# Fused image and text embedding, windowed attention and mixture of experts: products two slots later, routing in the next step, image rows earlier and partly on GpSimd

## The chip, the cores and the metric

The kernel runs on one core of a Trainium2 chip. The metric is device time in microseconds (us). Three runs of the kernel before gave 1399.01, 1400.30 and 1402.45 us, so the median is 1400.3 us. All profile times below are of one other execution, taken by the hardware profiler.

## The reference, cut to what matters

```python
h = clip(|x[i,j]-x[i+1,j+1]| + |x[i+1,j]-x[i,j+1]|, 0, 1)   # 16 images of 256 rows x 256
h = concat([h, table[x_txt]], axis=1)                       # + 77 text rows: S = 333 tokens of 256
h = h + attention(layernorm(h))                             # fp32 in, 16 heads of 16
h = h + experts(layernorm(h))                               # 8 experts, the 2 best, SwiGLU 256-512-256
```

The attention works on windows of 128 tokens at a stride of 64: four regular windows, and a fifth that ends at the last token. Each window has its own softmax over 128 keys with a position bias. The results of the windows that cover a token are added and divided by their number, and go through `Wo`. The experts take all 16 x 333 tokens together, sorted by expert.

## The kernel before

There are two stages. The **attention stage** goes over the 16 batches in steps: step `b` runs the attention of batch `b`, and beside it the projections of batch `b+1` (`proj`), the image, the text rows and the first layer norm of batch `b+2` (`inp`), the output projection, residual and second layer norm of batch `b-1` (`tail`), and the routing of batch `b-2` (`tail2`). The **expert stage** afterwards goes through 91 tiles of 128 sorted rows.

A step has 20 slots `k`: five windows times four groups of four heads. The order of the work is written out by hand. Every engine has its own function `step(b, par)` with a loop over `k`, in which lines such as `if proj and k == 4:` put a piece of side work into a slot. Engines run their own list strictly in order and meet at semaphores. A group goes through:

- PE, slot k: four score products of group k into `s_bank` (L1026); they need the row maxima of group k-2. At k = 0 the engine waits for `stack_in`, the landing of the batch's Q and K stacks.
- DVE, slot k: bias and row maximum of group k (L757, four instructions).
- ACT, slot k: exponential of group k-1 (L622), and then the copy of the transposed probabilities of group k-2 out of `t_bank` (L636). For every fourth group DVE makes that copy (L772, with the `weight` copy L776).
- PE, slot k: transpose of the probabilities of group k-3 (L1040), and their product with V for group k-4 (L1063). After a window's last group it transposes `weight` (L1072); ACT copies it (L642), DVE multiplies it into `head_out` (L784), and POOL adds that to `ctxT` (L520).

`probsT` has two buffers.

The Q and K stacks carry a chain of their own, from one step to the next. PE transposes the normalised rows `xn` of batch b+1 at k = 0 (L1082), ACT copies them (`xT`, L648), PE makes Q in slots 2 and 3 and K in slots 4 and 5 (L1104), and ACT takes each half out (`qk`, L660). Each of Q (n = 0) and K (n = 1) is then split into three bf16 parts: DVE rounds the first part (`part_high(n)`, L733), POOL subtracts (`split_rest(n)`, L502), DVE rounds the second (`part_middle(n)`, L738), and POOL subtracts again for the third (`split_last(n)`, L507). SP writes the parts to DRAM (L366) and reads them back, stacked by the products that are wanted, into `stacks` (L372): `load_stack(0)` for Q and `load_stack(1)` for K, six transfers of 166.5 KB each. SP's list is in order too:

```python
write_part(0, 2, part3_ready)
write_part(1, 1, part2_ready)
load_stack(0, q_stack[par1], Q_SLOTS)     # waits for all parts of Q in DRAM
write_part(1, 2, part3_ready)
if tail: store_h2()
load_stack(1, k_stack[par1], K_SLOTS)     # waits for all parts of K in DRAM
```

then four shifts inside V (L392 to L396), and the next step's image rows (L343 to L347).

Other side work that the texts name: `add_v` on DVE (L745, V out of PSUM), `moments_of` on DVE (L706 and L709, statistics of a layer norm, once for `inp` and once for `tail`), `inverse_root` on POOL (L472 to L484), `normalise` on DVE (L714, which makes `xn` for `inp`), the image's two differences on POOL (L533, L536) and their absolute values on DVE (L851), the sum and the clip on DVE (L870, L875), the output projection on PE (L1004) with the residual on DVE (L856), and the routing: gate product on PE (L1142), best two on DVE (L903 to L910), one-hot rows (L790 to L805), prefix sum on PE (L1089), places (L827 to L841) and scores (L812 to L819) on DVE, and six indirect scatters by POOL (L493).

## Time and profile before

| | |
|---|---|
| median of three runs | 1400.3 us (1399.01 to 1402.45) |
| profiled execution | 1394.69 us, span 1392.9 us |
| first scores of step 0 / step 1 / step 2 / step 15 | 63.43 / 116.21 / 162.03 / 786.04 us |
| first product of the expert stage | 872.3 us |
| busy over the span | PE 85%, DVE 66%, ACT 56%, POOL 44% |
| mean granted TensorE clock | 0.919 of full |

The span runs from the first to the last instruction. Times in the profile are from the span's start; the execution's own time is 1.8 us more than its span. L12 is line 12 of the kernel before. PEld is TensorE's weight load, which overlaps its products. SPq is the queue of transfers that SP issues. A bracket behind a row, as in [2.06 <-DMA stacks], is the idle time of the engine just before the row, and what ended it.

### The profile page before, as it was taken

Reading aid. Unit: us, or ns where it says so; the run is one execution under the profiler, and the core shown is the slowest. Engines: PE = TensorE matmul, PEld = TensorE weight load, DVE = VectorE, ACT = ScalarE, POOL = GpSimd, SP = SyncE. Lnnn points to the kernel's source line nnn. Section 1 sums busy time; section 2 is a strip of 40 time slices with the busy share of each in tenths; the row PEclk is TensorE's granted clock in tenths of the full one; section 3 lists DMA queues with packets and bytes.
Section 4 is the critical chain, followed back from the end, with each engine's and each line's share of the span. In section 5 each row is a group of like instructions: output and inputs, shape, how many; then the busy total and the mean of one; then the engine's idle time right before and its main releaser. Section 6 shows DMA issues by size and latency. Waiting matters only on the chain.

```text
span 1392.9 us, 35049 instructions
## 1 busy us (share of the span) xinstructions
PE 1189.1 (85%) x10190; PEld 951.8 (68%) x10191; DVE 920.9 (66%) x4211; ACT 782.9 (56%) x3176; POOL 611.8 (44%) x900
## 2 busy tenths in 40 slices
PE   2386888988988998888889872999999999999996
PEld 1254656655655665555556551999999999999995
DVE  4485989888888889898997864344444444444442
ACT  0196998989899998899899980211111111111110
POOL 5333466565646655665665334122322232232232
PEclk9698899889898988999998985899999999999998
DMA  3694563465357446634643507232233323323222
GB/s 110 133 234 100 109 132 89 95 131 113 88 103 142 92 92 116 128 89 94 133 107 71 96 24 234 36 50 46 49 47 48 49 45 49 48 46 48 46 49 31
DMA packets 98402, 123.36 MB, mean 89 GB/s; under 512 B 15544, under 2 KB 87416, under 8 KB 95192
## 3 DMA queue, kind: packets, MB, share of 16 engines
q1 hardware_dynamic: 75880, 89.96, 30.6%
q0 software_dynamic: 18576, 24.47, 10.9%
q10 hardware_dynamic: 3808, 7.34, 1.8%
q8 instruction: 57, 0.93, 0.3%
q14 instruction: 81, 0.66, 0.2%
HBM read 69.35 MB, written 46.07 MB: 83 GB/s over the span
## 4 chain that ended last, share of the span: by engine, by line
PE 47%; POOL 16%; issue 14%; DMA 12%; ACT 4%; SPq 3%; DVE 3%; POOLq 0%; DVEq 0%; ACTq 0%
PE s_bank L1168 12%; PE t_bank L1168 12%; PE o_bank L1183 11%; DMA qk_parts<-parts_flat 5%; POOL expert_slots L493 4%; DMA expert_slots<-rows,slot_i 4%; DMA stacks<-qk_parts 3%; PE m_bank L1104 3%; ACT probs L622 3%; PE t_bank L1040 2%; SPq L372 2%; POOL rest L502 2%; PE o_bank L1063 2%; POOL parts_flat L507 2%; PE m_bank L1157 1%
## 5 line engine op out<-in xcount | busy, mean ns | idle before, releaser
L622 ACT ACTIVATE probs<-probs,neg_max 128x128 f32<-128x128 f32 x1280 | 497.4, 401 | 21.6 <-DVE neg_max L757 21.0
L757 DVE CUSTOM_DVE_ANT_0 probs<-s_bank,nbias 128x128 f32<-128x128 f32 x1280 | 293.0, 284 | 38.4 <-PE s_bank L1026 36.9
L622 ACT ACTIVATION_READ_ACCUMULATOR probs<-probs,neg_max 128x1 f32 x1280 | 257.4, 201 | 0.0
L1040 PE MATMUL t_bank<-ident,probs 128*128 128x128 f32 x1280 | 221.0, 300 | 28.7 <-ACT probs L622 26.7
L681 ACT ACTIVATE v_all<-s_bank 128x512 f32<-128x512 f32 x91 | 54.4, 598 | 286.9 <-PE s_bank L1168 286.9
L1026 PE MATMUL s_bank<-stacks 96*128 96x128 bf16 x1280 | 136.5, 233 | 68.8 <-DMA stacks<-qk_parts 46.9
L1026 PEld LDWEIGHTS s_bank<-stacks 96*128 96x128 bf16 x1280 | 93.4, 105 | 132.4 <-DMA stacks<-qk_parts 50.7
L1040 PEld LDWEIGHTS t_bank<-ident,probs 128*128 128x128 f32 x1280 | 150.1, 153 | 45.7 <-ACT probs L622 41.7
L636 ACT ACTIVATE probsT<-t_bank 128x512 f32<-128x512 f32 x240 | 141.9, 591 | 57.5 <-PE t_bank L1040 56.7
L1183 PE MATMUL o_bank<-stacks,v_all 128*128 x728 | 172.6, 380 | 0.7 <-issue 0.5
L597 POOL DMA_INDIRECT out_dram<-wq_sb,nbias x46 | 75.7, 1645 | 198.5 <-DVE wq_sb L967 185.3
L1063 PE MATMUL o_bank<-probsT,v_all 128*32 128x128 f32 x2560 | 146.0, 303 | 16.9 <-ACT probsT L636 9.7
L597 POOL DMA_INDIRECT out_dram<-wk_sb,nbias x45 | 73.3, 1629 | 172.8 <-DVE wk_sb L967 170.0
L973 DVE TENSOR_TENSOR v_all<-v_all,t_bank 128x512 f32<-128x512 f32 x91 | 62.6, 688 | 127.1 <-PE t_bank L1168 127.1
L1183 PEld LDWEIGHTS o_bank<-stacks,v_all 128*128 128x128 f32 x728 | 131.3, 190 | 16.0 <-issue 1.8
L675 ACT ACTIVATE v_all<-m_bank 128x256 f32<-128x256 f32 x91 | 35.0, 384 | 143.3 <-PE m_bank L1157 143.3
L493 POOL DMA_INDIRECT expert_slots<-rows,slot_i x96 | 100.0, 1042 | 29.3 <-issue 21.7
L1063 PEld LDWEIGHTS o_bank<-probsT,v_all 128*32 128x32 f32 x2560 | 52.9, 112 | 79.0 <-issue 50.0
L757 DVE DVE_READ_ACCUMULATOR2_ANT neg_max<- 128x1 f32 x1280 | 103.8, 81 | 0.1
L1168 PEld LDWEIGHTS s_bank<-v_all,probs 128*128 128x128 f32 x736 | 91.0, 195 | 3.2 <-ACT v_all L675 0.9
L1168 PE MATMUL s_bank<-v_all,probs 128*128 128x128 f32 x736 | 91.4, 278 | 0.5 <-ACT v_all L675 0.5
L1168 PE MATMUL t_bank<-v_all,probs 128*128 128x128 f32 x736 | 90.7, 277 | 0.0
(158 smaller groups left out, 2079.4 us busy)
## 6 DMA issues: line engine op xcount, KB each, us to landing
stacks<-qk_parts SPq DMA_DIRECT2D x192, 166.5 KB, 5.6
qk_parts<-parts_flat SPq DMA_DIRECT2D x192, 83.2 KB
nbias<-expert_slots SPq DMA_DIRECT2D x91, 129.0 KB, 2.0
w_sb<-in_L_ffn_w_dram ACTq DMA_DIRECT2D x14, 512.0 KB, 5.2
v_all<-v_all SPq DMA_DIRECT2D x64, 96.0 KB, 6.4
x_here<-in_x_dram SPq DMA_DIRECT2D x16, 256.0 KB, 5.7
out_dram<-h_res SPq DMA_DIRECT2D x16, 256.0 KB
stacks<-in_L_ffn_w_dram SPq DMA_DIRECT2D x8, 512.0 KB, 8.5
```

What stands on the lines that cost most here:

```text
L493: pool.indirect_dma_start(slots_dram[:, :], bass.IndirectOffsetOnAxis(slot_i[0:n, kk, j:j + 1], 0), rows[0:n, kk, j, :], None).then_inc(sc ...
L597: pool.indirect_dma_start(out[:, :], bass.IndirectOffsetOnAxis(g_rows[r][:, D + 1:D + 2].bitcast(I32), 0), y_sb[r], None, compute_op=ALU.a ...
L622: ins = act.activation(seg, seg, ACT.Exp, bias=neg_max[:, r, i:i + 1], scale=-1.0, accum_out=row_sum[:, (par + v) % 2, h:h + 1])
L636: act.activation(probsT[:, k % 2, :], t_bank[:, k % 2, :], ACT.Copy).then_inc(pT_by_act, 1)
L681: act.activation(hidT[r % 2], s_bank[:, r % 2, :], ACT.Silu).then_inc(silu_ready, 1)
L757: ins = dve.tensor_tensor_reduce(probs[:, r, i * WIN:(i + 1) * WIN], s_bank[:, k % 2, i * WIN:(i + 1) * WIN], nbias[:, h, :], 1.0, BIG, AL ...
L973: dve.tensor_tensor(hidT[r % 2], hidT[r % 2], t_bank[:, r % 2, :], ALU.mult).then_inc(hid_ready, 1)
L1026: mm = pe.matmul(s_bank[:, k % 2, i * WIN:(i + 1) * WIN], q_stack[par][0:KROWS, h, lo:lo + WIN], k_stack[par][0:KROWS, h, lo:lo + WIN], st ...
L1040: mm = pe.transpose(t_bank[:, (k - 3) % 2, i * WIN:(i + 1) * WIN], probs[:, r, i * WIN:(i + 1) * WIN], ident[:, :])
L1063: mm = pe.matmul(o_bank[32 * i:32 * i + 32, vp, (g // 2) * WIN:(g // 2 + 1) * WIN], v_win[bp][:, w, c0:c0 + 2 * HD], probsT[:, (k - 4) % 2 ...
L1168: mm = pe.matmul(bank[:, par, n * P:(n + 1) * P], up_w[par][:, m, a, n * P:(n + 1) * P], gxT[par][:, a * P:(a + 1) * P], start=(a == 0), s ...
L1183: mm = pe.matmul(o_bank[:, r % 2, 0:D], hidT[r % 2][:, a * P:(a + 1) * P], w2_sb[:, bass.ds(e, 1), a, :].rearrange("p o n -> p (o n)"), st ...
```

## The change

It touches only the order of the attention stage, four buffers and two loads:

- The copies: ACT copies group k-3 at the head of slot k, ahead of the exponential of group k-1; DVE's copy of every fourth group moves one slot later, to the head of its slot. The product with V takes group k-6 instead of k-4. `probsT` has four buffers; the two new ones lie in the memory of the `w3` weights of expert 6, whose load moves from step 0 to the end of the attention stage. `head_out` and the `ctxT` additions move with the products.
- The routing of batch b-2: the gate product goes from slot 18 to slot 3 of the next step, the rest from slots 19, 0, 2, 3 to slots 4 (best two), 6 (one-hot rows), 9 (places) and 10 (scores); the scatters from slots 4 to 9 to slots 11 to 13.
- The image of batch b+2: POOL's differences at slots 0 and 1 instead of 2 and 3, DVE's absolute values at 2 instead of 7, sum and clip on POOL at 3 instead of on DVE at 11, moments at 5 instead of 15, the root at 12 instead of 16, `xn` at 16 instead of 18.
- The projections: the parts of Q and K one to two slots later, V directly behind K on PE (slots 6 and 7 instead of 10 and 11) and on DVE (8 and 9 instead of 12 and 14), the output projection at 10 and 11 instead of 6 and 7, residual, second layer norm and `x2T` two to four slots later.
- SP: the V shifts ahead of `load_stack(1)`, the store of h2 behind it.

```diff
-        probsT = sb("probsT", [P, 2, GH * WIN])
+        probsT2 = sb("probsT", [P, 2, GH * WIN])
+        probsT = [probsT2[:, i, :] for i in range(2)] + [w3_sb[:, E - 2, c, :] for c in range(C)]
...
                     load_stack(0, q_stack[par1], Q_SLOTS)
                     write_part(1, 2, part3_ready)
-                    if tail:
-                        store_h2()
-                    load_stack(1, k_stack[par1], K_SLOTS)
                     vt = v_win[par1]
...
                     sp.dma_start(vt[64:128, 3, :], vt[o:o + 64, 4, :]).then_inc(v_shift_in, 16)
+                    load_stack(1, k_stack[par1], K_SLOTS)
+                    if tail:
+                        store_h2()
...
+                    if inp and k == 3:
+                        pool.wait_ge(conv_step, b2 * 3 + 2)
+                        pool.tensor_tensor(diag[:, :, :], diag[:, :, :], anti[:, :, :], ALU.add).then_inc(conv_step, 1)
...
+                        pool.tensor_scalar(h_in[par][:, 0:2, :], diag[:, :, :], 1.0, 0.0, ALU.min, ALU.max)\
+                            .then_inc(image_ready, 1)
+                    if proj and k == 6:
+                        split_rest(0)
-                    if proj and k == 5:
-                        split_rest(0)
...
-                    if proj and k == 7:
+                    if proj and k == 8:
                         split_last(0)
                         split_rest(1)
...
-                    if proj and k == 9:
+                    if proj and k == 10:
                         split_last(1)
...
+                    g = (k - 3) % NG
+                    if g != 3 and ((k >= 3 and att) or (k < 3 and tail)):
+                        n = b * G + (k - 3)
+                        act.wait_ge(pT_done, n + 1)
+                        if n >= 4:
+                            act.wait_ge(pv_done, n - 3)
+                        act.activation(probsT[n % 4], t_bank[:, n % 2, :], ACT.Copy).then_inc(pT_by_act, 1)
                     if (k >= 1 and att) or (k < 1 and tail):
...
-                    if proj and k == 4:
+                    if proj and k == 5:
                         part_high(0)
-                    if proj and k == 6:
+                    if inp and k == 5:
+                        dve.wait_ge(image_ready, b2 + 1)
+                        dve.wait_ge(text_in, b2 * 16 + 16)
+                        if b2 >= 1:
+                            dve.wait_ge(rstd1_ready, b2)
+                        moments_of(h_in[par], stats1, moments1, b2, ln1_step)
+                    if proj and k == 7:
                         part_high(1)
+                    if proj and k == 8:
                         part_middle(0)
...
-                    if proj and k == 8:
+                    if proj and k == 10:
                         part_middle(1)
...
-                    if inp and k == 18:
+                    if inp and k == 16:
                         dve.wait_ge(rstd1_ready, b2 + 1)
...
-                    if (k >= 4 and att) or (k < 4 and tail):
+                    if (k >= 6 and att) or (k < 6 and tail):
 
-                        m, n = k - 4, b * G + (k - 4)
+                        m, n = k - 6, b * G + (k - 6)
...
-                    if tail and k == 18:
-                        pe.wait_ge(x2T_ready, b0 + 1)
-                        pe.wait_ge(head_ready, min(b * NW + 3, B * NW))
+                    if tail2 and k == 3:
+                        pe.wait_ge(x2T_ready, b9 + 1)
+                        pe.wait_ge(head_ready, min(b * NW - 1, B * NW))
```

On DVE the place that matters lies between the first rounding of K and its second. The rows are of the kernel before; each "..." stands for eight rows of the row maxima.

```order
L733 CAST parts_flat<-qk 128x2x333
L738 CAST parts_flat<-rest 128x2x333
...
L851 TENSOR_SCALAR diag<-diag 128x512
L851 TENSOR_SCALAR anti<-anti 128x512
...
L784 TENSOR_TENSOR head_out<-o_bank,weightT 128x256
L856 SCALAR_TENSOR_TENSOR h_res0<-m_bank,inv_count,h_res0 128x256 x2
L856 SCALAR_TENSOR_TENSOR h_res0<-m_bank,inv_count,h_res0 77x256
L738 CAST parts_flat<-rest 128x2x333
```

And the same place with the change, where lines are those of the changed kernel (L744 is `part_high`, L749 `part_middle`, L756 `add_v`, L850 and L854 begin the places, which go on over three more small rows, and L835 to L842 are the scores):

```order
L744 CAST parts_flat<-qk 128x2x333
...
L749 CAST parts_flat<-rest 128x2x333
L756 TENSOR_TENSOR v_all<-m_bank,bv_row 128x8x2x16 x2
...
L850 TENSOR_TENSOR place<-o_bank,region_end 128x24
...
L756 TENSOR_TENSOR v_all<-m_bank,bv_row 128x8x2x16
...
L790 RECIPROCAL inv_sum<-row_sum 128x16
L797 TENSOR_TENSOR head_out<-o_bank,weightT 128x256
L835 TENSOR_REDUCE score_sum<-score_e 128x3
...
L749 CAST parts_flat<-rest 128x2x333
```

Between the two roundings of K there were two groups of row maxima and now there are three; the V rows, the places and the scores have come in between, and the absolute values and the residual have gone.

On SP, the tail of the list of a step before:

```order
L372 DMA stacks<-qk_parts 16x5328 x6
L366 DMA qk_parts<-parts_flat 8x16x333 x2
L357 DMA out_dram<-h_res0 128x2x256
L358 DMA out_dram<-h_res0 77x256
L372 DMA stacks<-qk_parts 16x5328 x6
L392 DMA v_all<-v_all 64x384
```

and with the change:

```order
L373 DMA stacks<-qk_parts 16x5328 x6
L367 DMA qk_parts<-parts_flat 8x16x333 x2
L390 DMA v_all<-v_all 64x384
L391 DMA v_all<-v_all 64x384
L392 DMA v_all<-v_all 64x384
L394 DMA v_all<-v_all 64x384
L373 DMA stacks<-qk_parts 16x5328 x6
L358 DMA out_dram<-h_res1 128x2x256
```

The V shifts and the store of h2 have changed sides of the K stack.

## Rows read from the trace of the kernel before

**Rows 1.** Busy time by engine, attention stage (columns: us, busy, clock, DMA share, GB/s)

```profile
160.00:760.00 600.00, 525.76 (x4972) 359.79 (x4964) 528.16 (x2973) 539.38 (x2332) 353.18 (x598) 0.90 0.51 106
```

**Rows 2.** First scores of steps 1, 7, 8 and 15, PE in order of time

```profile
116.21 0.61 PE L1026 MATMUL s_bank<-stacks 96*128 96x128 bf16 x4 [12.46 <-DMA stacks<-qk_parts]
...
400.63 0.61 PE L1026 MATMUL s_bank<-stacks 96*128 96x128 bf16 x4 [1.36 <-DMA stacks<-qk_parts]
...
449.23 0.61 PE L1026 MATMUL s_bank<-stacks 96*128 96x128 bf16 x4 [2.06 <-DMA stacks<-qk_parts]
...
786.04 0.61 PE L1026 MATMUL s_bank<-stacks 96*128 96x128 bf16 x4 [1.73 <-DMA stacks<-qk_parts]
```

**Rows 3.** SP's queue in order of time, step 7

```profile
427.89 2.72 SPq L372 DMA_DIRECT2D stacks<-qk_parts  x6
430.65 1.22 SPq L366 DMA_DIRECT2D qk_parts<-parts_flat  x2
...
438.98 4.10 SPq L372 DMA_DIRECT2D stacks<-qk_parts  x6
```

**Rows 4.** The two stretches behind those issues, columns as in group 1

```profile
428.00:439.00 11.00, 8.49 (x87) 5.46 (x86) 10.97 (x59) 9.38 (x43) 6.66 (x18) 0.94 0.92 171
439.00:449.00 10.00, 8.09 (x86) 5.76 (x84) 7.91 (x46) 10.00 (x45) 5.68 (x17) 0.84 0.87 147
```

**Rows 5.** DVE in order of time, step 7

```profile
399.78 2.56 DVE L714 TENSOR_SCALAR xn<-h_in,moments,rstd 128x256 f32<-128x256 f32 x3 [2.10 <-POOL rstd L484]
...
411.85 0.18 DVE L827 TENSOR_TENSOR place<-o_bank,region_end 128x24 f32<-128x24 f32 x1
...
412.73 0.29 DVE L757 CUSTOM_DVE_ANT_0 probs<-s_bank,nbias 128x128 f32<-128x128 f32 x1
...
425.65 0.92 DVE L738 CAST parts_flat<-rest 128x666 bf16<-128x666 f32 x1 [0.37 <-POOL rest L502]
...
429.83 0.28 DVE L757 CUSTOM_DVE_ANT_0 probs<-s_bank,nbias 128x128 f32<-128x128 f32 x1
...
430.67 1.07 DVE L706 BATCH_NORM_STATS2 stats<-h_res 128x6 f32<-128x256 f32 x3
431.67 0.29 DVE L709 BATCH_NORM_AGGREGATE moments<-stats 128x2 f32<-128x6 f32 x3
```

**Rows 6.** PE in order of time, step 7, and the first of the expert stage

```profile
403.96 1.37 PE L1082 MATMUL m_bank<-ident,xn 128*128 128x128 f32 x6
...
422.14 0.61 PE L1040 MATMUL t_bank<-ident,probs 128*128 128x128 f32 x4
...
423.27 0.61 PE L1040 MATMUL t_bank<-ident,probs 128*128 128x128 f32 x4
...
444.25 1.33 PE L1142 MATMUL o_bank<-gate_sb,rest 128*128 128x8 f32 x12
...
871.17 0.66 PE L1157 MATMUL m_bank<-ident,nbias 128*128 128x128 f32 x2 [15.66 <-DMA nbias<-expert_slots]
```

**Rows 7.** DVE's groups, 160 to 760 us (busy us, mean ns of one; idle before)

```profile
L772 DVE COPY probsT<-t_bank 128x512 f32<-128x512 f32 x62 | 41.2, 664 | 22.5 <-PE t_bank L1040 22.2
L784 DVE TENSOR_TENSOR head_out<-o_bank,weightT 128x256 f32<-128x256 f32 x62 | 26.1, 421 | 9.3 <-ACT weightT L642 9.3
...
L745 DVE TENSOR_TENSOR v_all<-m_bank,bv_row 128x256 f32<-128x256 f32 x36 | 13.9, 414 | 0.0
```

**Rows 8.** Granted clock at the seam between steps and in slots 2 to 9

```profile
399.00:406.00 7.00, 4.36 (x31) 3.37 (x31) 6.15 (x34) 4.92 (x21) 3.10 (x5) 0.58 0.48 119
407.00:424.00 17.00, 17.00 (x168) 11.70 (x164) 13.69 (x85) 16.85 (x73) 10.62 (x10) 1.00 0.21 59
```

**Rows 9.** Waits by engine, 160 to 760 us (us in total, times, longest)

```profile
ACT probsT L636 <- PE t_bank L1040: 39.6, 50, 2.1
...
DVE xn L714 <- POOL rstd L484: 26.4, 13, 2.3
```

**Rows 10.** Software queue of transfers, 160 to 760 us

```profile
q0 software_dynamic: 4183, 9.58, 6.0%
```

More of the change, by code:

```diff
@@ L749, in step @@
                 for k in range(G):
+                    v = (k - 7) // NG
+                    if (k - 7) % NG == 0 and ((att and v >= 0) or (tail and v < 0)):
+                        n, wv, vp = b * G + (k - 4), b * NW + v, (par + v) % 2
+                        dve.wait_ge(pT_done, n + 1)
+                        if n >= 4:
+                            dve.wait_ge(pv_done, n - 3)
+                        dve.tensor_copy(probsT[n % 4], t_bank[:, n % 2, :]).then_inc(pT_by_dve, 1)
+                        dve.wait_ge(inv_ready, wv + 1)
+                        if wv >= 2:
+                            dve.wait_ge(weightT_done, wv - 1)
+                        dve.tensor_copy(weight[:, vp, :, :], inv_sum[:, vp, :].unsqueeze(2).to_broadcast([P, H, HD]))\
+                            .then_inc(weight_ready, 1)
                     if att:
@@ L785, in step @@
                             .then_inc(head_ready, 1)
-                    if tail2 and k == 0:
+                    if tail2 and k == 4:
+                        dve.wait_ge(logits_done, b9 + 1)
+                        dve.tensor_copy(logits[:, :, :], o_bank[:, par, 0:NT * E].rearrange("p (j e) -> p j e", j=NT))\
+                            .then_inc(logits_read, 1)
+                        dve.wait_ge(logits_read, b9 + 1)
+                        for j in range(NT):
+                            dve.max(best[:, j, :], logits[:, j, :]).then_inc(best_ready, 1)
+                        for j in range(NT):
+                            dve.wait_ge(best_ready, b9 * 6 + 1 + j)
+                            dve.max_index(best_i[:, j, :], best[:, j, :], logits[:, j, :]).then_inc(best_ready, 1)
+                    if tail2 and k == 6:
                         if b9 >= 1:
@@ L806, in step @@
                             .then_inc(taken_ready, 1)
-                    if tail2 and k == 2:
+                    if tail2 and k == 10:
                         dve.wait_ge(score_e_ready, b9 + 1)
@@ L822, in step @@
                         dve.wait_ge(token_step, b9 + 1)
-                    if tail2 and k == 3:
-                        counted = o_bank[:, par, 0:(NT + 1) * E]
+                    if tail2 and k == 9:
+                        counted = o_bank[:, 1 - par, 0:(NT + 1) * E]
                         dve.wait_ge(prefix_done, b9 + 1)
@@ L1083, in step @@
                         mm.then_inc(xT_done, 1)
-                    if tail2 and k == 2:
-                        counted = o_bank[:, par, :]
+                    if tail2 and k == 8:
+                        counted = o_bank[:, 1 - par, :]
                         pe.wait_ge(taken_ready, b9 + 1)
-                        pe.wait_ge(head_ready, min(b * NW - 1, B * NW))
+                        pe.wait_ge(head_ready, min(b * NW, B * NW))
                         pe.matmul(counted[:, 0:NT * E], before[:, :], taken[:, :, :].rearrange("p j e -> p (j e)"),
@@ L1106, in step @@
                         mm.then_inc(qk_done, 1)
-                    if tail and k == 6:
+                    if proj and k == 6:
+                        pe.wait_ge(qk_ready, b1 * 4 + 3)
+                        v_proj(0, 0, 0)
+                    if proj and k == 7:
+                        v_proj(0, D, 2)
+                        pe.wait_ge(qk_ready, b1 * 4 + 4)
+                        v_proj(1, 0, 4)
+                    if tail and k == 10:
                         pe.wait_ge(ctx_added, b0 * NW + NW)
                         if proj:
-                            pe.wait_ge(qk_ready, b1 * 4 + 3)
+                            pe.wait_ge(v_ready, b1 * 3 + 3)
                         elif b0 >= 1:
```

195 lines of the change are left out of this document (74 added, 121 removed).

## The prediction

> **What bounds the kernel now.** Read the attention stage first, as busy time by engine [rows 1]: of 600 us ACT is busy 539, DVE 528, PE 526. No engine is full, though each is within a tenth or so of it, and none names the bound. Next, who waits [rows 9]: ACT waits 39.6 us for transposes, DVE 26.4 us for the root on POOL. These invite the view that the engines are too tightly coupled, which is what longer distances and more buffers would cure. Then PE in order of time at the steps' seams [rows 2]: in the steps shown the first scores are released by the landing of the Q and K stacks, after 1.4 to 2.1 us idle, and 14 steps take 786.04 - 116.21 = 669.8 us, 47.85 each. The step's length is thus also that of a chain which runs from one seam to the next: xT, Q and K, their parts, the parts in DRAM, the stacks. In step 7 (from 400.63, 48.6 us long) its stations are, counted from the seam:
>
> - second rounding of K (`part_middle(1)`) ends on DVE at 425.65 + 0.92 = 426.57, so +25.9 [rows 2, 5];
> - the Q stack is issued at 427.89, so +27.3, which is 1.3 behind the rounding (the write of that part stands between) [rows 3];
> - the K stack is issued at 438.98, 11.1 us later [rows 3]; it waits for the last part of K, which is written behind the six Q transfers;
> - the next first scores are at 449.23, 10.25 us later [rows 2].
>
> In the last two stretches the transfer engines are 0.92 and 0.87 busy [rows 4]. From the Q stack on, the chain is therefore made of bytes: 11.1 + 10.25 = 21.3 us that no compute engine shortens. What the step can gain or lose through the chain, it gains or loses ahead of the Q stack, at `part_middle(1)`.
>
> **The change, part by part.** The question is when `part_middle(1)` ends, counted from a seam at which PE has waited for the stack and the other engines have caught up.
>
> *The start.* Before, `xn` is being normalised across the seam (until 402.34, 1.7 behind it) [rows 5], and PE's transposes of `xn` start at +3.3 [rows 6]. With the change `xn` is made in slot 16 and its root in slot 12; the 26.4 us of waits for the root (2.1 a step) go [rows 9]. I start xT at +2.0, 1.3 earlier. That is not all of the 3.3, since scores, transposes and product of slot 0 still stand ahead of it, and at the seam TensorE has its lower level of clock for part of the time: mean 0.58 of full against 1.00 in slots 2 to 9, of its two levels of 1.2 and 2.4 GHz [rows 8]. ACT, though, now has a `weight` transpose of PE's slot 1 to wait for ahead of its xT copy, so I expect only 0.5 to 1 us of it to reach Q.
>
> *PE up to slot 5.* A slot without side work costs PE 423.27 - 422.14 = 1.13 us [rows 6]. The gate product, 1.33 us [rows 6], now stands in slot 3, ahead of both halves of K. What was gained at the start is given back here: I put the scores of slot 5 at +13 (if the seam is at full clock) to +15 (at the lower level for slots 0 and 1).
>
> *DVE from slot 5 to `part_middle(1)`.* This is the term that counts. One group of maxima costs 430.67 - 429.83 = 0.84 us [rows 5]. Six of them (slots 5 to 10) are 5.0. Two roundings each of first and second parts at 0.5 are 2.0 (the row shows 0.92 for one beside a POOL subtraction) [rows 5]. The moments of the next image, new here, are 1.07 + 0.29 = 1.3 [rows 5]. The places of the routing, new here, take 412.73 - 411.85 = 0.9 [rows 5]; the one-hot rows and the scores, eleven small rows more, I estimate at 2.2 from that. V's three additions are 3 x 0.41 = 1.2, two head products 0.8 with two reciprocals of a quarter us, and one copy of `probsT` 0.66 [rows 7] with its small `weight` copy. That is 5.0 + 2.0 + 1.3 + 0.9 + 2.2 + 1.2 + 1.3 + 0.9 = 14.8, and 15.4 us with a few waits. So `part_middle(1)` ends at +28.4 to +30.4. I take +29.5, nearer the upper end since the seam of [rows 8] is at the lower clock, against +25.9: **3.6 us a step later**. The lower bound of the whole is 13 + 14.8 = 27.8, with no wait at all, 1.9 a step; the upper 30.9, with another half us of contention with POOL, 5.0. Less than that would take DVE or PE work away that the list still has there.
>
> *Behind it.* `split_last(1)` follows on POOL, which is freer than before since the scatters have gone behind it; its last part is written behind the Q stack in any case, so nothing is gained. SP's exchange of V shifts (4 x 96 KB) against h2 (333 KB) ahead of the K stack puts 51 KB more in front, about 0.3 us at 147 GB/s [rows 4]. I leave it in the range.
>
> *Covered.* Sum and clip on POOL take 1.15 us off DVE per step and cost POOL some 2 us in slot 3, where it has nothing due until slot 6. The longer distance of the products and the later copies remove ACT's waits for transposes [rows 9], 39.6 us in 12.5 steps, 3.2 a step, and DVE's for the root; but a step that is held by its stacks only turns them into a longer wait at its seam. If that cover goes, they are the gain of the first rival. The load of `w3` of expert 6 (0.5 MB) behind the stage joins 5 MB of expert weights that load beside the last routing; the expert stage starts on the landing of its token rows, not of its weights [rows 6]: nothing.
>
> *Sum.* 14 steps x 3.6 = +50. Step 15 prepares no batch and may gain its share of the waits: -1. On 1394.7 us, the profiled execution's own time, that is 1443.7; the median of the runs stands 5.6 higher, so I predict **1449 us**.
>
> **The rivals.**
>
> *A, the coupling was the bound (faster).* The stacks land in time and ACT sets the step: 539.4 of 600 us busy [rows 1] is 43.0 of 47.85, with 1.5 us of residual waits 44.5. 14 x -3.35 = -47: 1353 us. It decides if K's stack lands by +44.5, that is, if `part_middle(1)` ends before 44.5 - 21.3 - 1.3 = +21.9. For it: every engine has a tenth idle, and the root's wait is real. Against it: the rounding stands behind three groups of maxima and the routing instead of two. Chance 0.10.
>
> *B, no net change.* The earlier xT and the undisturbed DVE make up for the two slots, `part_middle(1)` stays near +25.9: 1400 us. Chance 0.05.
>
> *C, the scatters as well (slower still).* Six scatters move from slots 4 to 9 into slots 11 to 13, so into the two stretches that are 0.9 full [rows 4]; before, two of six lay there. Their queue takes 6.0% of all transfer engines [rows 10], 36 us in 12.5 steps, 2.9 a step with the text rows, some 0.45 per scatter. Four more are +1.8 us a step: 1449 + 25 = 1474 us. The Trainium skill (DMA: Bandwidth & Descriptors, section on queues, rings and completion order) says that each transfer engine takes turns between the queues that have work for it, a packet at a time. By that rule the scatters slow the stacks at once and are not served behind them; no row of the kernel before shows the two apart. Chance 0.25.
>
> *D, the forecast:* chance 0.60.
>
> **How the numbers follow.** The time is that of D. About 0.3% (4 us) is what a measurement of this kernel can tell from no change. A gives faster 0.10 and B a little of each side: faster 0.11, same 0.04, slower 0.85. The range takes D's bounds, 14 x 1.9 - 1 and 14 x 5.0 - 1 (1426 to 1469), C up to 1480, and below a part of B: 1410 to 1480. What is left out is A, half of B, and the end of C.
>
> **What would show it.** Right: every step's first scores released by the stacks, after more idle than 1 to 2 us; steps of 50 to 53 us; `part_middle(1)` ending at +28 to +31; Q stack to K stack still about 11 us and K stack to seam about 10; no wait of DVE for the root; ACT, DVE and PE less busy in share. Wrong: steps shorter than 47 us, or the first scores released by something other than a transfer. C would show as more than 22 us from the Q stack to the seam.

## The result and the profile after

The changed kernel takes **1460.6 us** (median; 1458.0 to 1463.6) against 1400.1 us before (median of four runs here; 1399.0 to 1402.5): a ratio of **1.043**, 95% interval 1.040 to 1.046. Slower, as forecast, and 11.6 us above the forecast of 1449. The profiled execution took 1461.98 us with a span of 1460.2; against the one before that is 67.3 us more, and all sums below are made against that.

The page of the kernel after, busy time by engine (PE's share includes the expert stage), and three of its rows of queues:

```profile
PE 1205.2 (83%) x10190; PEld 968.5 (66%) x10191; DVE 879.6 (60%) x4179; ACT 782.9 (54%) x3176; POOL 625.8 (43%) x932
...
q0 software_dynamic: 18576, 24.47, 10.9%
...
q8 instruction: 57, 0.93, 0.3%
q14 instruction: 81, 0.66, 0.2%
```

The attention stage, as in [rows 1]:

```profile
160.00:760.00 600.00, 496.07 (x4586) 344.20 (x4586) 457.18 (x2710) 498.18 (x2154) 332.34 (x572) 0.88 0.46 98
```

Every engine is less busy than in [rows 1], and so are the transfers (0.46 against 0.51): the same work per step is spread over a longer step, and the stage waits more. Where the time lies is read from PE in order of time, beside [rows 2] and the last of [rows 6]. First scores of steps 1, 7 and 8, those of slot 5 of step 7 between them, the first scores of step 15, and the first expert product:

```profile
117.51 0.61 PE L1030 MATMUL s_bank<-stacks 96*128 96x128 bf16 x4 [15.86 <-DMA stacks<-qk_parts]
...
424.68 0.61 PE L1030 MATMUL s_bank<-stacks 96*128 96x128 bf16 x4
...
437.50 0.39 PE L1030 MATMUL s_bank<-stacks 96*128 96x128 bf16 x4
...
476.31 0.61 PE L1030 MATMUL s_bank<-stacks 96*128 96x128 bf16 x4 [0.81 <-DMA stacks<-qk_parts]
...
840.78 0.40 PE L1030 MATMUL s_bank<-stacks 96*128 96x128 bf16 x4
...
938.89 0.45 PE L1157 MATMUL m_bank<-ident,nbias 128*128 128x128 f32 x1 [15.85 <-DMA nbias<-expert_slots]
```

The 67.7 us by which the expert stage begins later are 1.3 at the first seam, 723.3 - 669.8 = 53.4 in 14 steps (3.8 each), and 98.1 - 85.1 = 13.0 from the first scores of step 15 to the first expert product. From there to the end it is 521.3 us after and 521.7 before. (A seam is the moment at which a step's first scores begin.) Of the twelve seams at which steps 2 to 13 begin, seven show no wait of PE for a stack at all, as the one at 424.68. In the kernel before it was already five of twelve; [rows 2] has only seams with a wait.

What else holds them is seen in step 7, on four queues. SP's, beside [rows 3]:

```profile
454.31 2.71 SPq L373 DMA_DIRECT2D stacks<-qk_parts  x6
...
466.07 3.33 SPq L373 DMA_DIRECT2D stacks<-qk_parts  x6
```

DVE's, beside [rows 5]: second rounding of K, moments of the rows, and the rows themselves:

```profile
452.49 0.51 DVE L749 CAST parts_flat<-rest 128x666 bf16<-128x666 f32 x1
...
459.35 0.30 DVE L720 BATCH_NORM_AGGREGATE moments<-stats 128x2 f32<-128x6 f32 x3
...
465.99 1.11 DVE L725 TENSOR_SCALAR xn<-w_sb,moments,rstd 128x256 f32<-128x256 f32 x3
...
470.77 1.44 DVE L725 TENSOR_SCALAR rows<-h_res,moments,rstd 128x256 f32<-128x256 f32 x3 [2.26 <-POOL rstd L487]
```

POOL's: the last of the six scatters, then first and last instruction of the rows' root:

```profile
465.74 0.96 POOL L496 DMA_INDIRECT expert_slots<-rows,slot_i  x1 [0.30 <-issue]
466.76 0.38 POOL L475 TENSOR_SCALAR var_eps<-moments 128x3 f32<-128x3 f32 x1
...
470.54 0.19 POOL L487 TENSOR_TENSOR rstd<-rstd,root_tmp 128x3 f32<-128x3 f32 x1
```

And PE's transposes of the rows, in slot 18:

```profile
472.26 1.37 PE L1134 MATMUL m_bank<-ident,rows 128*128 128x128 f32 x6 [2.92 <-DVE rows L725]
```

Counted from the seam at 424.68: last rounding done at +28.3, stacks issued at +29.6 and +41.4, the next seam at +51.6. But the moments were ready at +35.0, and their root began only at +42.1: on POOL it stands behind three scatters, the next images' root (3.9 us) and three scatters more. Of the 7.1 us between, the images' root took the first part (it had begun at +34.4, when the first three scatters were off) and the last three scatters the rest. Rows at +46.1, transposes at +47.6, 4 us before the seam. That is a **second chain of almost the same length**, and it comes out in the waits of the stage:

```profile
DVE probs L780 <- PE s_bank L1030: 96.6, 96, 5.6
...
PE m_bank L1134 <- DVE rows L725: 32.8, 11, 5.3
ACT probsT L629 <- PE t_bank L1044: 31.6, 33, 3.6
...
DVE rows L725 <- issue: 20.3, 5, 4.9
...
ACT weightT L653 <- remote: 16.5, 7, 2.6
DVE rows L725 <- POOL rstd L487: 13.3, 6, 2.6
...
PE s_bank L1030 <- DMA stacks<-qk_parts: 8.8, 5, 5.2
```

Of [rows 9], DVE's wait for the root ahead of `xn` is gone. In its place DVE stands at the rows, 33.6 us in all, PE behind it for 32.8, and the stacks account for 8.8 alone. The 20.3 us with the releaser "issue" show no partner; the last experiment shows what they are.

### The profile page after: what moved, and what is told of

The parts are those of the page before. It is cut to its first block, busy times and chain, and to the rows that moved or that the text cites. A ratio compares the mean times of both kernels' runs of the same rounds, so it can differ in the third digit from the quotient of the medians.

```text
span 1460.2 us, 35047 instructions
## 1 busy us (share of the span) xinstructions
PE 1205.2 (83%) x10190; PEld 968.5 (66%) x10191; DVE 879.6 (60%) x4179; ACT 782.9 (54%) x3176; POOL 625.8 (43%) x932
## 4 chain that ended last, share of the span: by engine, by line
PE 56%; POOL 11%; issue 11%; ACT 6%; DMA 6%; DVE 5%; SPq 4%; another core or an unknown queue 1%; ACTq 0%; POOLq 0%; DVEq 0%
PE s_bank L1168 11%; PE t_bank L1168 11%; PE o_bank L1183 11%; PE t_bank L1044 5%; PE m_bank L1108 4%; POOL expert_slots L496 4%; ACT probs L638 4%; PE o_bank L1067 3%; DMA stacks<-qk_parts 3%; DMA qk_parts<-parts_flat 3%; PE m_bank L1015 3%; PE s_bank L1030 2%; SPq L373 2%; PE m_bank L1157 1%; PE o_bank L1142 1%
## 5 line engine op out<-in xcount | busy, mean ns | idle before, releaser
L1044 PE MATMUL t_bank<-ident,probs 128*128 128x128 f32 x1280 | 230.9, 310 | 64.9 <-ACT probs L638 60.1
L1044 PEld LDWEIGHTS t_bank<-ident,probs 128*128 128x128 f32 x1280 | 156.9, 159 | 85.2 <-ACT probs L638 77.0
L1030 PE MATMUL s_bank<-stacks 96*128 96x128 bf16 x1280 | 140.8, 238 | 55.4 <-DMA stacks<-qk_parts 49.2
L1030 PEld LDWEIGHTS s_bank<-stacks 96*128 96x128 bf16 x1280 | 100.0, 107 | 105.7 <-DMA stacks<-qk_parts 53.5
L629 ACT ACTIVATE probsT<-t_bank 128x512 f32<-128x512 f32 x160 | 94.9, 593 | 68.3 <-PE t_bank L1044 55.5
L496 POOL DMA_INDIRECT expert_slots<-rows,slot_i x96 | 96.6, 1006 | 37.8 <-issue 29.2
L510 POOL TENSOR_TENSOR parts_flat<-rest,parts_flat 128x666 bf16<-128x666 f32 x32 | 45.2, 1412 | 110.5 <-DVE parts_flat L749 110.5
L1168 PEld LDWEIGHTS s_bank<-v_all,parts_flat 128*128 128x128 f32 x720 | 87.4, 192 | 3.0 <-ACT v_all L686 0.7
```

The costliest lines, as they stand in the source:

```text
L496: pool.indirect_dma_start(slots_dram[:, :], bass.IndirectOffsetOnAxis(slot_i[0:n, kk, j:j + 1], 0), rows[0:n, kk, j, :], None).then_inc(sc ...
L629: act.activation(probsT[n % 4], t_bank[:, n % 2, :], ACT.Copy).then_inc(pT_by_act, 1)
L1030: mm = pe.matmul(s_bank[:, k % 2, i * WIN:(i + 1) * WIN], q_stack[par][0:KROWS, h, lo:lo + WIN], k_stack[par][0:KROWS, h, lo:lo + WIN], st ...
L1044: mm = pe.transpose(t_bank[:, n % 2, i * WIN:(i + 1) * WIN], probs[:, r, i * WIN:(i + 1) * WIN], ident[:, :])
L1168: mm = pe.matmul(bank[:, par, n * P:(n + 1) * P], up_w[par][:, m, a, n * P:(n + 1) * P], gxT[par][:, a * P:(a + 1) * P], start=(a == 0), s ...
```

## The experiments

Theory S (the prediction's): the chain to the stacks sets the step, and the roundings lengthened it. Theory T: the tail does, that is product with `Wo`, residual, moments, root, rows, transposes in slot 18. For orientation, the means over steps 2 to 13 of each kernel in us, from its timeline, counted from the seam (the last rounding is `part_middle(1)`; "K to seam" goes from the issue of K's stack to the next seam):

```text
kernel                         step  last rounding  K stack  K to  rows' root  rows
                                      ends           issued  seam  starts      start
before                         48.0   25.9           38.2     9.8  31.4        38.0
after                          51.9   28.7           41.3    10.6  42.5        47.3
before, roundings late         49.8   27.5           40.1     9.7  30.0        35.6
before, routing late           52.9   28.6           41.9    11.0  34.8        45.0
before, images ahead           47.0   24.3           37.4     9.6  29.8        36.2
after, roundings early         50.8   23.0           36.3    14.4  40.1        46.5
after, root in slot 14         52.3   28.2           41.3    11.0  38.1        48.0
after, root in slot 8          51.9   29.0           42.0     9.9  39.9        46.9
  and roundings early          51.2   24.1           36.7    14.5  40.9        47.2
after, routing early           48.2   25.9           38.9     9.4  36.7        40.6
  and roundings early          46.6   22.6           36.2    10.4  35.6        39.6
  and images as before         46.3   23.1           36.4     9.9  35.4        40.1
  or scatters late again       51.2   22.2           35.4    15.8  37.6        44.0
```

**1. The roundings alone, on the kernel before.**

```diff
-                    if proj and k == 4:
+                    if proj and k == 5:
                         part_high(0)
...
-                    if proj and k == 8:
+                    if proj and k == 10:
                         part_middle(1)
```

(`part_high(1)` 6 to 7, `part_middle(0)` 6 to 8; GpSimd's slots 5, 7, 9 to 6, 8, 10.)

> The kernel before with one thing of the change alone: the roundings of Q and K one to two slots later on DVE (first parts in slots 5 and 7, second parts in 8 and 10) and the subtractions on GpSimd in slots 6, 8, 10; nothing else moves. Theory S (the step is set by the chain to the stacks, and its loss is the two slots of the last rounding): part_middle(1) ends at about +30 instead of +25.9, Q stack at about +31.5, each step 3.5 to 4.5 us longer, 1450 to 1463 us. Theory T (the step after the change is set by the tail: product with Wo, moments, root on GpSimd, rows, transposes of rows in slot 18): the tail of this kernel is where it was, so the Q and K stacks only come later into slack: under 1 us a step, 1400 to 1414 us.

Measured: 1423.4 us, ratio 1.016 (1.013 to 1.019). It falls between the two bands: the direction is S's, the size less than half. PE now stands at each seam for its stack:

```profile
PE s_bank L1027 <- DMA stacks<-qk_parts: 69.3, 12, 6.8
```

With 5.8 us of waiting at the seam the next step begins with everyone caught up: xT starts at +2.0 instead of +3.2 and the scores of slot 5 at +12.4 instead of +13.7, and the two slots cost 1.7 us at the last rounding, not the 4.8 of two slots of 48.0 / 20 us.

**2. The roundings back, in the kernel after.** The same edit the other way.

> The kernel after with the roundings of Q and K and their subtractions back in the slots of before (4, 6, 6, 8 on DVE and 5, 7, 7, 9 on GpSimd), the rest as changed. S: part_middle(1) ends 3 to 4 us earlier, near +25.5, and the step follows: 47.5 to 48.5 us, 1401 to 1416 us. T: the stacks land early, but TensorE still stands at the transposes of the rows in slot 18 and the step keeps at least 50.5 us: 1445 to 1461 us. If both chains are nearly equally long, the step falls by only part of it, to 49.5 to 50.5: 1430 to 1444 us.

Measured: 1434.6 us, 1.025 (1.022 to 1.028); 26 us of the loss, in the band for two chains of about one length. The last rounding ends at +23.0 and K's stack is issued at +36.3, so by the 9.4 to 9.9 us that it takes where a stack releases the seam it has landed at +46, yet the seam comes at +50.8. The same waits as above:

```profile
PE m_bank L1134 <- DVE rows L725: 65.0, 11, 6.7
...
DVE rows L725 <- issue: 66.8, 10, 7.3
```

At the twelve seams that end its steps 2 to 13 PE never waits for a stack. The tail alone holds this kernel at 50.8. S by itself is refuted.

**3. The next images' root moved behind the rows' root** (GpSimd, slot 12 to slot 14), without and with the early roundings.

```diff
-                    if inp and k == 12:
+                    if inp and k == 14:
...
                         inverse_root(moments1, rstd1, root1_step, b2, rstd1_ready)
```

> The kernel after with one move: the root for the next images (GpSimd, slot 12) put behind the root for the rows (slot 14), so that the rows' root stands behind 3.8 us less of GpSimd work. S: the wait of the transposes in slot 18 (34.4 us in 12.5 steps) falls under 15, but the first scores wait for the stacks instead: 1455 to 1461 us. T: the step falls by 1 to 2 us, 1432 to 1447 us.

> Both of the moves: roundings back in their slots of before and the next images' root behind the rows' root. S: as with the roundings alone, within 5 us. T: as with the root alone, within 5 us. Two chains of nearly one length: this one gains clearly more than the sum of the two kernels with one move each, down to 1385 to 1410 us.

Measured: 1462.8 us, 1.045 (1.043 to 1.046), and 1441.8 us, 1.030 (1.028 to 1.032). Neither time lies in a band of any theory, because the move was badly chosen: on DVE `xn` stands in slot 16, ahead of the rows in 17, and now waited for its own late root. The rows' root began at 38.1 instead of 42.5 and the rows at 48.0 instead of 47.3. It decides nothing between the theories, except that a root is not late alone: whoever queues behind its reader is late too.

**4. The same root moved ahead instead** (slot 8), without and with the early roundings.

```diff
-                    if inp and k == 12:
+                    if inp and k == 8:
...
                         inverse_root(moments1, rstd1, root1_step, b2, rstd1_ready)
```

> The kernel after with one move: the root for the next images goes from GpSimd's slot 12 to slot 8, behind the subtractions of that slot and so out of the queue in which the rows' root stands (the last kernel with a moved root put it where the next images' normalisation, and behind it the rows, waited for it: no test of the tail). Two-chain theory: the rows' root ends 3 to 4 us earlier, the wait of the row transposes in slot 18 (34.4 us in 12.5 steps) falls under 10, and the step is then that of the stacks alone, 50.5 to 51.5 us: 1445 to 1458 us. Stacks alone (theory S): no change, 1457 to 1463. Landing theory (the rows wait for the landing of the scatters and not for the root): the wait in slot 18 stays above 20 us and the time is unchanged.

> The kernel after with the roundings and subtractions back in the slots of before and the next images' root behind the subtractions of slot 7. Two-chain theory: both chains are now shorter, neither holds the step above 48.5 us: 1390 to 1416 us, most of what the change lost. S: as with the roundings alone, 1434 us. Landing theory: the wait in slot 18 falls by less than half of its 65 us, 1425 to 1435 us.

Measured: 1461.2 us, 1.047 (1.044 to 1.050), and 1448.0 us, 1.037 (1.035 to 1.039). In the first, PE's wait for the rows fell from 32.8 us to 1.0, as the two-chain theory had it, but the time did not move, and with early roundings it rose by 13 us. The gap on POOL had closed, so that all six scatters follow one another beside the stacks, and a new idle time stands there on three engines (PE's in small pieces). The waits with early roundings:

```profile
ACT weightT L653 <- remote: 62.3, 11, 5.8
DVE probs L780 <- remote: 53.1, 10, 6.0
```

In step 5 of that kernel (seam at 315.52; scatters issued from 345.85 on) the scores and the transposes that the two wait for were done by 349.2:

```profile
353.37 0.29 DVE L780 CUSTOM_DVE_ANT_0 probs<-s_bank,nbias 128x128 f32<-128x128 f32 x1 [4.57 <-remote]
...
354.95 0.38 ACT L653 ACTIVATE weightT<-o_bank 128x256 f32<-128x256 f32 x1 [5.69 <-remote]
```

The queues at 348 to 349, 349 to 350 and 350 to 351 us (packets, MB, share of 16 engines):

```profile
q1 hardware_dynamic: 41, 0.08, 60.1%
...
q1 hardware_dynamic: 124, 0.11, 76.5%
q8 instruction: 1, 0.02, 10.3%
...
q1 hardware_dynamic: 233, 0.18, 72.7%
q0 software_dynamic: 22, 0.07, 28.9%
```

From 345 to 350 us no packet of the scatters moved, while q1 was 60 to 116% busy in each microsecond, and one packet of the instruction queue moved where the stall begins. What is waited for no row shows (see the last section). For the first kernel S had given the right time (1457 to 1463), but experiment 2 had refuted it; its time for the second, 1434, was 14 us off. The landing theory failed in the first, where it wanted a wait of over 20 us in slot 18. The two-chain theory had the wait right, but its gain did not come. That the stall took its place is my reading of the waits; no run removes the stall alone.

**5. Parts of the change alone, on the kernel before.** The routing four slots further (gate product in slot 2 of the next step, scatters in 8 to 13; the counting bank changes to the other of the two):

```diff
-                    if tail and k == 18:
-                        pe.wait_ge(x2T_ready, b0 + 1)
+                    if tail2 and k == 2:
+                        pe.wait_ge(x2T_ready, b9 + 1)
...
-                    if tail2 and k == 9:
+                    if tail2 and k == 13:
                         scatter(1, 2)
```

> The kernel before with the routing of a batch four slots further alone (gate product in slot 2 of the next step, places in 7, scores in 6, scatters on GpSimd in slots 8, 9, 10, 10, 12, 13); copies, products, images and roundings stay. If the late scatters are what makes the tail: the rows' root (slot 11) stands behind a scatter less or more, but the rows (slot 14) wait for scatters issued in slot 13 and land 3 us or more later, and the transposes of the rows (slot 16) wait 2 to 6 us a step; the stacks keep their time (+38, +48), so the step grows by 0 to 2 us: 1400 to 1428 us. If only the roundings and the queue of roots matter: within 1395 to 1407.

Measured: **1472.4 us**, 1.053 (1.050 to 1.056), slower than the whole change; far above the band. DVE stands at the rows:

```profile
DVE rows L714 <- issue: 58.8, 11, 6.7
```

Here the root can't be what they wait for. The end of the rows' root and the rows, in step 2:

```profile
202.59 0.19 POOL L484 TENSOR_TENSOR rstd<-rstd,root_tmp 128x3 f32<-128x3 f32 x1
...
210.79 1.06 DVE L714 TENSOR_SCALAR rows<-h_res,moments,rstd 128x256 f32<-128x256 f32 x3 [6.67 <-issue]
```

In steps 2 to 13 the rows begin 4.9 to 8.0 us after their root is done, but only 0.6 to 1.8 us after the last packet of the software queue, which carries the scatters.

The tail was expected and is there, but the step is 4.9 longer instead of 2: the routing's work also pushes the last rounding from +25.9 to +28.6, 1.5 of it already by slot 5 of PE (+15.2 instead of +13.7).

The image rows ahead (differences in 0 and 1, sum and clip on GpSimd in 3, moments in 5, root in 12, `xn` in 16):

```diff
+                    if inp and k == 3:
...
+                        pool.tensor_tensor(diag[:, :, :], diag[:, :, :], anti[:, :, :], ALU.add).then_inc(conv_step, 1)
...
-                    if inp and k == 18:
+                    if inp and k == 16:
                         dve.wait_ge(rstd1_ready, b2 + 1)
```

> The kernel before with the image rows ahead alone: differences on GpSimd in slots 0 and 1, signs in slot 2 and moments in slot 5 on DVE, sum and clip on GpSimd in slot 3, root in slot 12, normalisation in slot 16. It takes the wait at the seam (xT at +3.3 comes to +2) and the sum and clip from DVE, and adds 1.3 us of moments ahead of the roundings: part_middle(1) at +25 to +26.5, 1375 to 1408 us. Were this part the one that costs, 1410 us or more.

Measured: **1381.4 us**, 0.989 (0.987 to 0.992): a gain, near the lower end of the band, since the last rounding ends at +24.3, earlier than I gave it.

**6. The routing four slots earlier in the kernel after**, so one slot behind before; this undoes the shift and keeps the rest, except that the rows and their transposes go one slot earlier too (16 and 17), to leave the gate product its place.

```diff
-                    if tail2 and k == 3:
-                        pe.wait_ge(x2T_ready, b9 + 1)
+                    if tail and k == 19:
+                        pe.wait_ge(x2T_ready, b0 + 1)
...
-                    if tail2 and k == 13:
+                    if tail2 and k == 9:
                         for j in range(NT):
                             scatter(1, j)
```

> The kernel after with the routing of a batch four slots earlier, so one slot behind where it was before (gate product in slot 19, logits in slot 0, places in 5, scores in 6, scatters on GpSimd in slots 7, 8, 9 instead of 11, 12, 13), and rows and their transposes one slot earlier (16, 17) to leave the gate product its copy. Roundings stay late, images early, copies and products late. Two-chain theory: scatters and routing are what makes the tail, the stacks stay: no wait for rows, no stall beside the scatters, the step is that of the stacks alone, 49 to 50.5 us: 1422 to 1445 us. If the routing's place does not matter: 1455 to 1463.

Measured: 1409.1 us, 1.0055 (1.004 to 1.008). Below the band: 51.5 of the 60.4 us are gone, because the stack chain is shorter as well: the roundings are in the slots of the change, yet the last ends at +25.9 instead of +28.7. I put the 2.8 us down to the routing's work on PE and DVE, which left slots 3 to 10: 0.4 of them are there at slot 5, 2.4 come behind it.

With the roundings back too:

```diff
-                    if proj and k == 10:
+                    if proj and k == 8:
                         part_middle(1)
```

> The same with the roundings and subtractions of Q and K back in the slots of before. Two-chain theory: part_middle(1) ends near +24, the stacks land near +46, the tail is clear of them: 46 to 47.5 us a step, 1372 to 1400 us; all of the loss is then placed. If the later copies and products, or the images, cost something themselves: above 1410 us.

Measured: **1382.2 us**, 0.987 (0.984 to 0.989). And with the images on before's engines and slots again. What is left of the change is a bundle: the later copies and products with their four buffers, SP's order, V's projection earlier, the output projection, residual and second layer norm two to four slots later, and the routing one slot later:

```diff
-                    if inp and k == 3:
-                        pool.wait_ge(conv_step, b2 * 3 + 2)
+                    if inp and k == 11:
+                        dve.wait_ge(conv_step, b2 * 3 + 2)
```

> The same with the images back in the slots and on the engines of before: of the change only the later copies and products, their four buffers and SP's order are left. If they gain what the waits between the engines promised (ACT 39.6 us in 12.5 steps): 1370 to 1390 us. If the stacks hold the step anyway: 1392 to 1410 us.

Measured: 1381.1 us, 0.986 (0.984 to 0.988). This bundle gains 20 us, the images alone 16, and both together 19, no more than either. No run takes the bundle apart, so which of its parts gains is open. In neither version does PE wait for a stack at more than four of the seams; the step's next limit is elsewhere. In the version with both, the stage reads

```profile
160.00:760.00 600.00, 528.40 (x5121) 364.51 (x5122) 512.12 (x3033) 555.20 (x2409) 369.23 (x642) 0.93 0.52 111
```

ACT is busy 555 of 600 us, 43.1 of a step of 46.6, and PE's largest wait is for it:

```profile
PE t_bank L1044 <- ACT probs L638: 43.9, 56, 2.7
```

These three kernels (images alone, the bundle alone, both) beat the kernel before and the change; they can't be told apart.

**7. Only the scatters late.** The last question was which part of the routing costs the 51.5 us: its work on DVE and PE, or the six scatters. In the version with both, the scatters alone go back to the change's slots:

```diff
-                    if tail2 and k == 7:
+                    if tail2 and k == 11:
                         pool.wait_ge(slots_ready, b9 + 1)
...
-                    if tail2 and k == 9:
+                    if tail2 and k == 13:
                         for j in range(NT):
                             scatter(1, j)
```

> The fastest kernel with the change's later copies and images (routing one slot behind before, roundings early: 1382 us) with one more move: only the six scatters on GpSimd go to the slots that the change gave them (11, 11, 12, 13, 13, 13 instead of 7, 7, 8, 9, 9, 9); gate product, places and scores on PE and DVE stay early. If the scatters' place alone makes the tail (they stand ahead of the rows' root on GpSimd and land late beside the stacks, and DVE waits at the rows for both): the rows start 4 to 7 us later, the step grows from 46.5 to 49.5 to 51 us, 1424 to 1446 us; that is nearly all of the 52 us by which routing four slots back shortened this kernel. If it is the routing's work on DVE and PE (3 us ahead of the last rounding) that costs the 52: 1380 to 1392 us.

Measured: 1443.5 us, 1.032 (1.028 to 1.037): **61 us for the place of six scatters** (64 by the two ratios), within the band. The kernel of experiment 2, in which the routing's work on PE and DVE is late as well, takes 1434.6, no more: with the scatters late and the roundings early, the place of that work costs nothing. The stacks are early (K's issued at +35.4); all of it is tail:

```profile
DVE rows L725 <- issue: 53.8, 11, 6.0
...
PE m_bank L1134 <- DVE rows L725: 50.2, 11, 6.9
```

In its step 2 (seam at 161.90), the last scatter, the end of the rows' root, and the rows:

```profile
198.70 0.96 POOL L496 DMA_INDIRECT expert_slots<-rows,slot_i  x1 [0.30 <-issue]
...
203.34 0.19 POOL L487 TENSOR_TENSOR rstd<-rstd,root_tmp 128x3 f32<-128x3 f32 x1
```

```profile
206.65 1.06 DVE L725 TENSOR_SCALAR rows<-h_res,moments,rstd 128x256 f32<-128x256 f32 x3 [5.36 <-issue]
```

The software queue in 204 to 205 and 205 to 206 us (between them the other queues); in 206 to 207 it moved nothing:

```profile
q0 software_dynamic: 21, 0.02, 14.7%
...
q0 software_dynamic: 1, 0.00, 0.2%
```

The root is done at 203.53, the last packet of the scatters moves at 205, and the rows begin at 206.65: they overwrite the buffer that the scatters read (`dve.wait_ge(scattered, b0 * 96)`), and the last scatter, off POOL at 199.66, needed over 5 us to land beside the stacks. In steps 2 to 13 the rows begin 0.7 to 1.6 us after that queue's last packet, and 0.4 to 3.9 us after their root (2.5 in the mean). With experiment 5 this settles it: "issue" at the rows is the landing of the scatters. They cost twice: 3 x 1.3 us of POOL ahead of the root, and 2.5 us behind it.

## Why the prediction was right, and where it was not

- **xT at +2.0**: 1.8 in the mean. **Scores of slot 5 at +13 to +15**: 437.50 - 424.68 = +12.8 in step 7. **DVE from there to the last rounding 14.8 to 15.4 us**: 453.00 - 437.50 = 15.5. The mean is 15.5 too. Its routing share, 0.9 + 2.2 = 3.1 us, was somewhat large: in experiment 6 this stretch is 2.4 us shorter.
- **Last rounding at +29.5**: +28.7. 2.8 us later than before, where I gave 3.6; the scores of slot 5 come at +13.2, near the lower end of the +13 to +15 that I had put.
- **Behind it**: Q stack 1.3 later, as put; Q to K 11.4 (11.1); K to seam 10.6 (10.25). Where a stack releases the seam it is 9.8 to 10.2; what the others have above that (up to 12.6) is PE still held by slot 18.
- **3.6 us a step**: 3.8. The sum over 14 steps, 53.4 against 50, agrees partly by luck: the term of the roundings was 0.8 too large, and behind it come 0.8 more from K's stack to the seam, most of it at seams where PE is held by slot 18, and 0.4 from Q to K; the prediction had neither. And the term itself isn't what the step would give back: with the roundings early again 26 of the 60 us go, since the tail, which the prediction lacks, holds the step at 50.8 without them.
- **"Step 15 may gain: -1"** failed: from its first scores to the first expert product it took 13.0 us more. Its row transposes stand at +44.9 (885.67) instead of +34.0 (820.02). I had treated the end as free of the chain. But the expert stage begins on the landing of the last scatters, and POOL issues the last one 92.1 us after the first scores of step 15 instead of 77.7; the routing four slots later alone, in experiment 5, makes this end 15.7 us longer. Against the profiled execution the forecast was 1462.0 - 1443.7 = 18.3 us short: 14 here, 3.4 in the 14 steps, 1.3 at the first seam (18.7, and -0.4 in the expert stage). That the one profiled execution lies 5.6 below its median and the other 1.4 above takes the miss to 11.3, and the rounding of the forecast to 11.6.
- **"Every step's first scores released by the stacks"** failed: at seven of twelve seams they were not, which was my own mark for being wrong. The premise was weak already: I read it from the seams of [rows 2], and five of twelve show no such wait in the kernel before. The step that failed is the one under "Behind it": I counted POOL as "freer than before since the scatters have gone behind" the last subtraction, and asked of the scatters only what they take from the stacks. I did not follow what is queued behind them on POOL (the rows' root), nor what waits for their landing (the rows).
- **Rival C** had the right place, the scatters in the full stretches, and missed the main victim. Its mark was over 22 us from the Q stack to the seam; that is 21.9 in the mean, and where it is clearly more (23.1 to 23.3), the seam was not released by a stack. The stacks did come somewhat later, 0.7 to 1.3 us where C put 1.8 (see the last section). But the six places alone cost 4.7 a step in experiment 7, where PE waits for no stack at the seams that end steps 2 to 13.
- **Rival A** was refuted here only because the last rounding was late. In experiment 6, where it ends at +22.6, near the +21.9 that I had asked for, a gain appears, 19 us of the 47 that I gave it; ACT is then busy 43.1 us of each step, as A has it (43.0).
- **Expert stage nothing**: 521.3 against 521.7 us.

As measured, with the medians: the bundle of experiment 6 with the early images -19, the roundings one to two slots later +27 (1382 to 1409), the routing four slots further +51.5 (1409 to 1461). The last two add, whichever comes first: with the roundings early the routing costs 52 (1382 to 1435, experiment 2), and with the routing late the roundings cost 26. Of two chains of which only the longer counts one would expect less than the sum. The rows say why it is not so: each move lengthens both chains. Late roundings delay the moments on DVE (ready at +36.4 against +34.3 with them early), and the routing delays the rounding by 2.8. SP's new order was never tried alone and stays open; so does how the cost of the late scatters splits between POOL's queue and the landing.

## What to carry to other kernels

When work is moved off one chain, follow what queues behind it on its new engine and which buffer it keeps: a scatter is 1.3 us of GpSimd and its source stays locked until it lands, which beside full transfers took over 5 us. Look for a second chain within a few per cent of the first before trusting the first; here, taking either off alone left a loss. When a bundle loses, take it apart: the images ahead gain 16 us by themselves, and what is left without images, late roundings and late routing gains 20.

## What the runs showed of the hardware

With six indirect scatters issued back to back beside the stacks, DVE and ACT stop for 5 to 6 us once a step (experiment 4), with no releaser that belongs to the kernel ("remote" is another core or an unknown queue); with the same six in two groups and a root between them, as in the change, ACT does so for 16.5 us in 600. In the two kernels of experiment 3 six follow one another too and no such row appears, but there DVE stands at `xn` for the root, 6 to 7 us in most steps, so a stall could hide in that wait. The cause is open. A candidate is the loading of instructions. The Trainium skill (Runtime: NRT & Kernel Launch, section on instruction fetch mechanics) says that each engine's sequencer fetches its code by a DMA queue of its own, in blocks of 16 KiB, and that this is mostly hidden. The trace agrees in part: of its two instruction queues q8 moved 0.93 MB in 57 packets, 16.3 KB each, and q14 0.66 MB in 81, 8.1 KB each. But the candidate does not carry the stall: in five of ACT's eleven stalls of the last kernel of experiment 4 no packet of either instruction queue moved from 2 us before the stall to 2 us after it.

In the step shown in experiment 4 the scatters' first packet moved over 4 us after their first issue, while q1 was 60 to 116% busy. With the routing and the roundings early, where the first scatter is issued ahead of the stacks, it is 1.6 to 1.9 us in every step from 2 to 13; in the last kernel of experiment 7, beside the stacks, 2.8 to 5.7. The rule of the Trainium skill that the prediction set beside rival C (DMA: Bandwidth & Descriptors, section on queues, rings and completion order), by which a transfer engine takes turns between the queues packet by packet, did not show in that stretch; the trace does not tell when the scatters' descriptors were there to be served, so it isn't refuted. By that rule the stacks should have been slowed, and something of it is there. Taken over the seams of steps 3 to 14 at which PE waits for a stack, the time from the Q stack's issue to the seam is 20.5 us with early scatters (routing early, 11 seams) and with late ones 21.8 (after, 4 seams) and 21.3 (root in slot 8, 8 seams): 0.7 to 1.3 us more. These kernels differ in more than the scatters, so this is an estimate.
